# A vision tower with routed experts: shared chunks, slot numbers and closing rows in a new order

## What is computed

```python
h = embed(x)                                   # 64 images, 37 tokens each, 256 wide: 2368 rows
h = layernorm(h + attention(h))                # 16 heads, contextual positions (CoPE)
scores = softmax(h @ router_w)                 # 8 experts
topk_scores, topk_idx = top_k(scores, 2)
routed = sum over the two: score * ((silu(h @ gate_w[e]) * (h @ up_w[e])) @ down_w[e])
shared = silu(h @ shared_gate_w) * (h @ shared_up_w) @ shared_down_w      # 512 wide
out = layernorm(h + shared + routed)
```

## Time and profile before

| | |
|---|---|
| median of 3 runs | 790.96 us (787.9 to 791.86) |
| the profiled execution's own time | 790.15 us |
| its span, first to last instruction | 788.4 us |
| busy share of the span | PE 93%, DVE 68%, ACT 53%, POOL 20% |
| mean granted TensorE clock | 0.964 of full |
| attention, to the first 8-column router product | 0 to 496.88 us |
| routing and shared chunks 0 to 5 ahead of the tiles, with the loop's first products | 496.88 to 607.9 us |
| tiles, to the last down product | 607.9 to 730.9 us |
| shared chunks 6 to 9 and closing rows | 730.9 to 788.4 us |

### The profile page before, as it was taken

The page is one execution under the profiler, slowest core; times in us unless marked ns, Lnnn a source line. Parts: engine busy times, 40 slices in busy tenths (PEclk is TensorE's granted clock), DMA queues, the critical chain, the costliest instruction groups (busy, mean ns, idle before and its releaser), DMA issues. The chain is left out here.

```text
span 788.4 us, 14542 instructions
## 1 busy us (share of the span) xinstructions
PE 735.5 (93%) x5009; PEld 638.7 (81%) x5010; DVE 539.5 (68%) x1135; ACT 419.5 (53%) x779; POOL 159.2 (20%) x200
## 2 busy tenths in 40 slices
PE   5988999999999999999999979998988999999991
PEld 5867697979798897979797957886867999999881
DVE  0069898989798898979898988962651444444673
ACT  2365847565756758575756556211113555554254
POOL 2000000000000000000000000006743677775222
PEclk9999999999999999999999989788999999999986
DMA  8930001010102010010000033000001222221611
GB/s 286 313 127 25 11 24 45 23 45 23 45 0 66 2 51 18 23 34 23 12 23 12 16 116 105 24 22 19 0 3 44 75 86 82 80 87 42 247 67 57
DMA packets 28302, 47.35 MB, mean 60 GB/s; under 512 B 4793, under 2 KB 19107, under 8 KB 28274
## 3 DMA queue, kind: packets, MB, share of 16 engines
q1 hardware_dynamic: 22802, 37.24, 14.5%
q0 software_dynamic: 5472, 9.76, 4.0%
HBM read 35.57 MB, written 13.24 MB: 62 GB/s over the span
## 5 line engine op out<-in xcount | busy, mean ns | idle before, releaser
L572 POOL TENSOR_TENSOR rs<-ve,neg_half 111x2 f32<-111x2 f32 x11 | 12.4, 1130 | 491.3 <-DVE ve L1463 491.3
L743 PE MATMUL ps_X<-wkv_sb,hT 128*111 128x512 f32 (+1 forms) x176 | 85.7, 619 | 7.9 <-ACT v_sb L1115 7.4
L998 PE MATMUL ps_S<-attnT,v_sb 128*128 128x128 f32 x704 | 86.0, 275 | 1.3 <-ACT attnT L1237 0.8
L1382 DVE COPY_PREDICATED table<-bit,table 111x112 f32<-111x112 int16 (+6 forms) x110 | 76.3, 694 | 11.4 <-DVE table L1382 0.2
L998 PEld LDWEIGHTS ps_S<-attnT,v_sb 128*128 128x128 f32 x704 | 82.2, 192 | 1.8 <-ACT attnT L1237 1.0
L1066 ACT COPY simS<-ps_S 32x666 f32<-32x666 f32 (+3 forms) x105 | 74.1, 705 | 13.5 <-DVE table L1439 10.6
L743 PEld LDWEIGHTS ps_X<-wkv_sb,hT 128*111 128x111 f32 (+1 forms) x176 | 27.9, 174 | 50.7 <-issue 30.1
L1708 DVE COPY attnT<-ps_S 128x256 f32<-128x256 f32 x44 | 18.7, 424 | 71.1 <-PE ps_S L1012 71.1
L684 PE MATMUL ps_S<-hT,wq_sb 128*128 128x222 f32 (+1 forms) x352 | 66.3, 345 | 0.0
L684 PEld LDWEIGHTS ps_S<-hT,wq_sb 128*128 128x128 f32 x352 | 63.5, 190 | 0.1
L781 PE MATMUL ps_X<-oT,wout_sb 128*128 128x222 f32 x320 | 61.9, 350 | 0.0
(11 more groups left out here) (208 smaller groups left out, 1438.1 us busy)
## 6 DMA issues: line engine op xcount, KB each, us to landing
down_sb<-in_x_dram SPq DMA_DIRECT2D x10, 648.0 KB
gu_sb<-y_d SPq DMA_DIRECT2D x8, 512.0 KB, 6.9
h_d<-hT SPq DMA_DIRECT2D x11, 222.0 KB, 2.5
kept<-h_d SPq DMA_DIRECT2D x11, 222.0 KB, 2.6
h_d<-h SPq DMA_DIRECT2D x10, 222.0 KB
wkv_sb<-in_L_attn_Wkv_dram SPq DMA_DIRECT2D x2, 1024.0 KB, 10.2
gu_sb<-in_L_ffn_gate_w_dram SPq DMA_DIRECT2D x2, 1024.0 KB, 11.2
gu_sb<-in_L_ffn_up_w_dram SPq DMA_DIRECT2D x2, 1024.0 KB, 12.2
```

Source lines behind the costliest of these rows:

```text
L743: mm = nc.tensor.matmul(X[:r, 1 - s], hT[:, k].rearrange("p b t -> p (b t)")[:, a * ROWS:a * ROWS + r], wkv_sb[:, k, INNER + 512 * s:INNER ...
L998: mm = nc.tensor.matmul(S[:, i, j * FF + f * P:j * FF + f * P + P], held[:, i, k, j, f * P:f * P + P], xgT[:, i, k], start=(k == 0), stop= ...
L1382: A.did(V.copy_predicated(near[:, :, :, 0:SL - d], by_side(bit[:, n], r)[:, :, :, 0:SL - d], near[:, :, :, d:SL]))
```

## The change

- **Order of chunks.** `ORDER` is 0 to 5, then the small chunk 9, then 6, 7, 8; `AT[c]` is a chunk's place in it and replaces c in every wait. Chunk 9 is now ahead of the tiles. ScalarE's weights copy for tile 0 waits for the down product of chunk 5 alone, that for tile 1 for chunk 9's.
- **Routing inside the last pair.** `warm` issues a matmul of 512 columns whose result nobody reads: one behind the routes of chunks 1, 3 and 5, two ahead of the last group's transpositions.
- **Last residual.** It is cut in two halves with `rank(0)` between them; chunk 7 is turned and routed, and a step of the shared expert of chunk 0 done, around `by_tokens`. On VectorE `slots(0)` stands right behind the last residual, ahead of `norm1`.
- **GpSimd.** The zeroing of `xg` comes first; then the first two scatters, the last pair's `norm`, and the other 36 scatters.
- **Second routing batch.** Chunks 8 and 9 are turned ahead of chunk 2, routed between its steps; `slots(1)` is two chunks earlier in VectorE's order.
- **One Silu pass.** From chunk 3 on (`LATE`) and for all tiles, ScalarE applies Silu in place of Tanh, and VectorE multiplies by the up half in one operation in place of two. ScalarE's Silu of a chunk also waits for VectorE's step f - 2, since its buffer is read directly. Behind the change the compiler places one more ACT_TABLE_LOAD, in front of chunk 3's first Silu, and no other.
- **Closing rows.** The loads, rows, norms and stores follow `ORDER`: 14 blocks within the steps of chunks 7 and 8, the table being 0, 1, 1, 4 and 1, 1, 1, 5, and five behind. The store loops, GpSimd's scale loop and ScalarE's closing part change in the same sense only.

The diff, cut to its core:

```diff
@@ -392,13 +392,23 @@
             eng.nop(nofuse=True)
-        BEFORE = 6
+        ORDER = [*range(FULL - 1), NCH - 1, *range(FULL - 1, NCH - 1)]
+        AT = {c: at for at, c in enumerate(ORDER)}
+        BEFORE = FULL
+        LATE = 3
         N_TABLES = 8
+        row_order = [PER * c + n for c in ORDER for n in range(chunks[c][2])]
+        ROW_AT = {half: at for at, half in enumerate(row_order)}
         rows_at, so_far = [], 0
-        for n in [0] * FC + [1, 1, 1, 2] * 2 + [0, 0, 0, 5]:
-            rows_at.append(list(range(so_far, so_far + n)))
+        for n in [0] * FC + [0, 1, 1, 4] + [1, 1, 1, 5]:
+            rows_at.append(row_order[so_far:so_far + n])
             so_far += n
-        LATER = range(so_far, NROW)
+        LATER = row_order[so_far:]
+        def closed(half):
+            return half == row_order[-1] or half // PER != row_order[ROW_AT[half] + 1] // PER
         ROUTED = X[:, 1]
         def turned_in(c):
@@ -577,11 +589,13 @@
             nc.gpsimd.tensor_copy(ids[:], ids_f[:]).then_inc(ids_numbered, 1)
             norm(0)
-            with pool.Fori(1, G2) as p:
+            with pool.Fori(1, G2 - 1) as p:
                 norm(p)
             pool.wait_ge(ids_zeroed, 16)
             pool.wait_ge(ids_numbered, 1)
+            pool.wait_ge(at_done, 4 * G)
+            nc.gpsimd.memset(xg[:], 0.0).then_inc(xg_zeroed, 1)
             def scatter(b, tiles):
@@ -614,9 +628,9 @@
                                              y_sb[:, b], None, bounds_check=TOPK * REAL - 1, oob_is_err=False
                                              ).then_inc(tile_stored[b], 16)
-            scatter(0, range(FIRST))
-            pool.wait_ge(at_done, 4 * G)
-            nc.gpsimd.memset(xg[:], 0.0).then_inc(xg_zeroed, 1)
+            scatter(0, range(1))
+            norm(G2 - 1)
+            scatter(0, range(1, FIRST))
             scatter(1, range(FIRST, NROW))
             pool.wait_ge(tiles_ready, 1)
             pool.wait_ge(ids_stored, 16 * TOPK * NROW)
@@ -772,15 +787,19 @@
...
+            def residual_half(p, bank, m):
...
+                for f in range(FT):
+                    mm = nc.tensor.matmul(bank[:, m * COLS:m * COLS + w], wout_sb[:, f, m * P:(m + 1) * P],
+                                          oT[:, f, :w], start=(f == 0), stop=(f == FT - 1))
+                return mm
...
-                for m in range(KE):
-                    for f in range(FT):
-                        mm = nc.tensor.matmul(bank[:, m * COLS:m * COLS + w], wout_sb[:, f, m * P:(m + 1) * P],
-                                              oT[:, f, :w], start=(f == 0), stop=(f == FT - 1))
-                mm.then_inc(res_done, 1)
+                residual_half(p, bank, 0)
+                residual_half(p, bank, 1).then_inc(res_done, 1)
@@ -849,9 +868,14 @@
...
+                    pe.wait_ge(sh_hid, AT[c] * FC + f - 1)
...
+            def warm(n, to):
+                for _ in range(n):
+                    nc.tensor.matmul(to, ones[:, :], sgu_sb[:, 0, 0].rearrange("p j f -> p (j f)"), start=True, stop=True)
@@ -897,6 +921,8 @@
...
+                        elif c < FULL - 1:
+                            warm(1, S[:, 2])
@@ -938,41 +964,51 @@
             def shared_out(c):
                 _, parts, per = chunks[c]
-                pe.wait_ge(sh_hid, c * FC + FC)
+                pe.wait_ge(sh_hid, AT[c] * FC + FC)
                 if c == 0:
                     pe.wait_ge(h1_ready, 2 * G2 + 2)
                 else:
-                    pe.wait_ge(sh_rec, c)
+                    pe.wait_ge(sh_rec, AT[c])
                 for n in range(per):
                     for f in range(FC):
-                        mm = nc.tensor.matmul(S[:parts, 2 + n, :EMB], hidS[:, c % 2, f, n * P:n * P + parts],
+                        mm = nc.tensor.matmul(S[:parts, 2 + n, :EMB], hidS[:, (AT[c] + 1) % 2, f, n * P:n * P + parts],
                                               sdown_sb[:, f], start=(f == 0), stop=(f == FC - 1))
                 mm.then_inc(sh_down, 1)
+            def lists_turned():
+                pe.wait_ge(lists_num, 1)
+                nc.tensor.transpose(E[:, 1, :NT], lists_f[:NT, :], ident[:NT, :NT]).then_inc(lists_t, 1)
+            warm(2, S[:, 2])
             turn_weights(G - 1, False)
             outputs(G - 1, 1)
-            residual(G2 - 1, S[:, 2])
+            pe.wait_ge(ot_sb, 2 * G)
+            residual_half(G2 - 1, S[:, 2], 0)
+            rank(0, 0, FIRST)
+            residual_half(G2 - 1, S[:, 2], 1).then_inc(res_done, 1)
+            turn(FULL)
+            shared_hidden(0, 2, 3)
             by_tokens(G2 - 1, S[:, 3])
-            rank(0, 0, FIRST)
-            shared_hidden(0, 2, FC)
+            route(FULL)
+            shared_hidden(0, 3, 4)
             shared_hidden(1)
-            turn(FULL)
-            route(FULL)
             shared_out(0)
-            for c in range(FULL + 1, NCH):
-                turn(c)
-                route(c)
-            shared_hidden(2)
+            turn(FULL + 1)
+            turn(FULL + 2)
+            shared_hidden(2, 0, 1)
+            route(FULL + 1)
+            route(FULL + 2)
+            shared_hidden(2, 1, 2)
             shared_out(1)
             rank(1, FIRST, NROW)
-            for c in range(3, BEFORE - 1):
+            shared_hidden(2, 2, 4)
+            for c in range(3, FULL - 1):
                 shared_hidden(c)
                 shared_out(c - 1)
-            shared_hidden(BEFORE - 1)
-            pe.wait_ge(lists_num, 1)
-            nc.tensor.transpose(E[:, 1, :NT], lists_f[:NT, :], ident[:NT, :NT]).then_inc(lists_t, 1)
-            shared_out(BEFORE - 2)
-            shared_out(BEFORE - 1)
+            lists_turned()
+            shared_hidden(NCH - 1)
+            shared_out(FULL - 2)
             def transpose_x(t, turn, b):
                 pe.wait_ge(tile_x[b], turn * 16 + 16)
@@ -1017,9 +1053,8 @@
             pe.wait_ge(w_exp, N_W_EXP)
             pe.wait_ge(tiles_named, 1)
             pe.wait_ge(ids_ready, 2)
-            pe.wait_ge(sh_hid, BEFORE * FC)
-            pe.wait_ge(sh_rec, BEFORE)
             transpose_x(0, 0, 0)
+            shared_out(NCH - 1)
             transpose_x(1, 0, 1)
             gate_up_tile(0, 0)
             transpose_x(2, 0, 2)
@@ -1213,7 +1248,12 @@
...
+                if c >= LATE:
+                    if f >= 2 or c > LATE:
+                        act.wait_ge(sh_hid, AT[c] * FC + f - 1)
+                    nc.scalar.activation(thS[:, f % 2, :w], S[:, f % 2, :w], ACT.Silu).then_inc(sh_tanh, 1)
@@ -1221,16 +1261,22 @@
             router_exp(0, 0, FIRST)
             weights(G - 1, 2, 4)
             outputs(G - 1, 1)
-            for c in range(2):
+            for f in range(2):
+                shared_tanh(0, f)
+            turn(FULL)
+            for f in range(2, FC):
+                shared_tanh(0, f)
+            for f in range(FC):
+                shared_tanh(1, f)
+            turn(FULL + 1)
+            turn(FULL + 2)
+            shared_tanh(2, 0)
+            router_exp(1, FIRST, NROW)
+            for f in range(1, FC):
+                shared_tanh(2, f)
+            for c in ORDER[3:BEFORE]:
                 for f in range(FC):
                     shared_tanh(c, f)
-            for c in range(FULL, NCH):
-                turn(c)
-            for c in range(2, BEFORE):
-                for f in range(FC):
-                    shared_tanh(c, f)
-                    if c == 2 and f == 1:
-                        router_exp(1, FIRST, NROW)
             def x_in_sbuf(t, i):
                 act.wait_ge(tile_xt, t + 1)
@@ -1239,7 +1285,7 @@
...
-                nc.scalar.activation(thg[:, i], S[:, i, :FF], ACT.Tanh, scale=0.5).then_inc(tile_tanh, 1)
+                nc.scalar.activation(thg[:, i], S[:, i, :FF], ACT.Silu).then_inc(tile_tanh, 1)
@@ -1266,9 +1312,9 @@
...
-            act.wait_ge(sh_down, BEFORE)
...
+                act.wait_ge(sh_down, BEFORE - 1 + t)
@@ -1600,17 +1646,21 @@
...
+                if c >= LATE:
+                    V.tensor_tensor(hidS[:, (AT[c] + 1) % 2, f, :w], thS[:, i, :w], S[:, i, CHUNK:CHUNK + w], ALU.mult
+                                    ).then_inc(sh_hid, 1)
+                    return
@@ -1668,38 +1718,38 @@
             for f in range(2):
                 shared(0, f)
             residual(G2 - 1, S[:, 2])
+            slots(0, 0, FIRST)
             norm1(G2 - 1, S[:, 3], 0)
             shared(0, 2)
             norm1(G2 - 1, S[:, 3], 1)
             shared(0, 3)
-            shared(1, 0)
-            slots(0, 0, FIRST)
-            for f in range(1, FC):
+            for f in range(FC):
                 shared(1, f)
             shared_sum(0)
-            for c in range(2, BEFORE):
+            choose(1, FULL, NCH, FIRST, NROW)
+            for f in range(2):
+                shared(2, f)
+            slots(1, FIRST, NROW)
+            shared(2, 2)
+            shared_sum(1)
+            shared(2, 3)
```

(32 more changed lines are left out.)

65 lines of the change are left out of this document (33 added, 32 removed).

## The result

The changed kernel takes 786.9 us (median of 19 runs, 782.4 to 790.5); the kernel before, beside it, 789.88 (19 runs). The ratio is 0.9955, 95% interval 0.9942 to 0.9967: 3.6 us won where 14.5 were forecast. The profiled execution is one of the slowest, 790.15 us with a span of 788.4, the same as that of the profile before the change.

A forecast was written before the change was run, and what follows sets the result against it. TensorE bounds the tiles, idles and loses clock in the first stretch; VectorE's rows set the end. Gains 9.5 + 0.45 + 4.5 = 14.5 off 790.15 give 775.7, stated as 775.5; range 771 to 784.

The forecast's parts named there:

- no wait: Ahead of the tiles: TensorE would not wait for loads of chunks 8 and 9, with 4.6 us left for their transfer.
- the first stretch: From the attention's end at 496.88 to the tiles at 607.9: 101.5 us against 111.0, 9.5 us won.
- Clock held by the fillers: First stretch: five filler products, 4.4 us of work, keep TensorE's clock full where it fell at 503.2, which cost 8.
- Wait for the norm, 2.4: First stretch: TensorE newly waits 2.4 us for step 3 of chunk 0, since the norm stands behind two scatters.
- No wait for the lists: Ahead of the tiles: lists come near 581.0, TensorE reaches them at 583, so the 3.8 us wait is gone.
- Silu: Tile loop: at Tanh's price (383 ns) it gains only 0.45 us, behind the last tile; its table load is hidden.
- Zeroing beside the choice: First stretch, near 512.5: GpSimd's zeroing beside VectorE's choice costs nothing, at most 0.96 us.
- Behind the tiles: After the tile loop: VectorE's rows end at 42.2 us, ScalarE at 46.0; 4.5 us won, bounds 3 and 6.5.
- clock falls all the same: Ahead of the tiles: TensorE's clock falls in thin places anyway; one or two falls give 777.5 to 781; chance 0.27.
- the rivals: Clock falls ahead of the tiles 0.27, closing rows gain nothing 0.1, moves cancel 0.04, slower through dear Silu 0.04.

The follow-up runs named there:

- the best kernel: The changed kernel with the last norm ahead of all scatters and the turns and routes of chunks 8 and 9 later: 772.67 us against 789.09, ratio 0.979.
- the changed kernel's second profile: The changed kernel run again unedited beside the kernel before, with stalls: 814.25 us against 821.02, ratio 0.9911.

## Why the prediction was wrong

The step that failed is the one on the last norm's rows: "their loads, issued at 532.98, are then issued near 534, and TensorE wants them at 538.6. That leaves 4.6 us for the transfer; I count no wait, and whatever they take above it is one." It took the 5.3 us from stores to loads from a trace in which no scatter ran then (the first at 533.98, after the loads' issue) and, by its own numbers, moved the scatters (524.4) to some 4 us ahead of the stores (behind VectorE's norm, which it had end near 528.9). The loads were issued at 540.94 and landed at 547.6 and 549.7. So the term "no wait" is 7.4 us, and in the trace the low clock that followed (17.1 us, half of its 13.35 busy, 6.7) nearly doubles it. The kernels without scatters and with the norm ahead show that the transfers slowed by running scatters come first and the norm's own lateness second; the kernel with the loads covered shows what the wait and the clock behind it were worth.

In the trace the 15.8 us by which the first stretch misses its 101.5 are: 7.4 of this wait, 6.7 of the clock behind it, 3.2 of the clock around the half residual (half of 6.42), 0.8 of other work (0.65 of it the attention's), less 2.4 of other waits that were counted and came out smaller.

The other steps, one by one:

- *Clock held by the fillers*: right for the routes, wrong for the half residual, which took 4.31 us instead of 2.1 in a low clock from 514.2 to 521.0. So the first scatter came at 527.14, not 524.4 (0.65 of that is the attention's). The low clock there lasted only 3.4 us in the best kernel, whose first scatter is at 526.09. Where the loads are covered, the fillers are worth 1.5 us by the medians, if anything; the forecast had 8 - 4.4 = 3.6.
- *Wait for the norm, 2.4*: it was 1.99.
- *No wait for the lists*: right in the changed kernel, but only because TensorE was late. The lists were cast by 586.8, not 581.0, since the first scatter was 2.7 us late and GpSimd then stood 4.8 us for the slots of the second batch (chunks 8 and 9, late with their loads); TensorE came only at 599.45. In the best kernel the forecast holds: TensorE is there at 581.88, 1.4 us behind their arrival.
- *Silu*: right. Its mean is 0.384 us, Tanh's was 0.383, and the loop's 123.0 became 122.53, by 0.47 (forecast 0.45). The groups of the changed loop, and the table load:

```profile
L1752 DVE TENSOR_TENSOR q<-gate,ps_S 128x256 f32<-128x256 f32 x43 | 17.8, 413 | 0.4 <-ACT gate L1288 0.4
...
L1288 ACT ACTIVATE gate<-ps_S 128x256 f32<-128x256 f32 x43 | 16.5, 384 | 45.1 <-PE ps_S L1034 45.1
```

```profile
568.87 1.28 ACT L1255 ACT_TABLE_LOAD   x1
570.20 0.38 ACT L1255 ACTIVATE ex<-ps_S 128x256 f32<-128x256 f32 x1
```

  The first Silu starts 0.05 us behind the load's end. The drain of about 1.4 us that the Trainium skill (ScalarE: Activation LUTs, What ACT_TABLE_LOAD costs) adds is not seen here, and the load was hidden.
- *Zeroing beside the choice*: right at nothing. The memset runs from 513.28 to 514.23, and the choice ends 0.69 us later than before, 0.65 of which is the attention's. The Trainium skill's contention (GPSIMD Engine Reference, Key points), for VectorE instructions with two SBUF inputs, was not put to the test: beside the memset VectorE ran a reduction and a reciprocal, with one input each, and its next operation with two starts at 514.18.
- *Behind the tiles*: right. The down product waited 5.00 and took 5.35 (forecast over 5 and 5.4). VectorE's last row ends 42.2 us behind the loop (778.83 - 736.67; forecast 42.2), ScalarE 45.3 (forecast 46.0), and the stretch lost 5.8 us against 4.5 forecast, inside the bounds of 3 and 6.5. VectorE's last row and ScalarE's last operation:

```profile
778.68 0.15 DVE L1789 TENSOR_SCALAR neg_mean<-resT 128x1 f32<-128x1 f32 x1
```

```profile
780.83 1.09 ACT L1345 ACTIVATE down_sb<-wq_sb,shift,rsc 128x256 f32<-128x256 f32 x2 [0.38 <-POOL shift L665]
```

Two small slips in the readings change nothing: the choice ends at 517.46 by its row, not 517.36, and the steps from 529.7 to the turns add up to 538.4, not 538.6.

The rival "clock falls all the same" did come about, once where it said, in the thin place from 511 to 517 (3.2 us lost), and once behind a wait that it didn't have. None of the rivals had the transfers themselves slower. With that mended by order alone, 772.7 us stand against the 775.5 forecast. That this is so near is partly luck: its first stretch takes 99.7 us instead of 101.5, and the tail gives 1.3 us more than forecast.

## What to carry to other kernels

When a change lets a stream of small indirect transfers start earlier, list the transfers it will now run beside, and take their price from a place in the trace where the two overlap, not from where they stood alone. A round trip through DRAM on which another engine waits is best covered by putting its consumer behind work that is ready: that brought 0.012 of the time here, some 9 us, where making its producer earlier brought 3 by the medians, which the noise covers. And a wait can cost more than itself: behind the two longest waits for the loads here the clock was low for 17.1 and 6.8 us.

## What the runs showed of the hardware

- Beside running scatters of at most 128 words each, 1.26 us apart, two plain stores of together 148 KB took 7.4 to 9.4 us from their issue to the next load's (fourteen profiles), and 5.2 or 5.3 without a scatter in flight (six). The load of 256 KB landed 6.0 to 9.1 us after its issue (the five such profiles without stalls) instead of 2.7 or 2.8. The loads' 224 packets took 60 us of the DMA engines' time instead of 18, while the scatters' own packets took 1.8% of the 16 engines' time. What in the chip they share is not shown: they are in different queues.
- Not every wait of TensorE brings the clock down. In the changed kernel's trace the 1.99 us wait for the norm's step left it at full; in that of the kernel with the loads covered the same wait, 2.00 us, was followed by about 3.4 us at the low level.
- In the runs with stalls the computing engines stood again and again, TensorE for 14 to 22 of the 35 us from 540 to 575 and 14 to 18 us more over the tile loop (141.2 to 145.1 instead of 126.8 to 127.8), in every order of the work. Holding the scatters back moved these stalls with them (waits of 20.3 and 15.1 us from 549 on). ScalarE and VectorE were released late there, as in this row of the changed kernel's second profile: ScalarE's copy of transposed rows starts at 551.89, where TensorE had done the transpositions by 544.6 ("remote" is the profile's word for a release that it finds at no engine of the core):

```profile
551.89 0.58 ACT L1181 COPY kT<-ps_X 128x512 f32<-128x512 f32 x1 [14.66 <-remote]
```

  What makes these stalls is open, and whether it is the chip; the kernel before itself has no profile with them, only its order with Silu stands for it, and no run without scatters fell on them.
